# Five padded count matmuls in another bank, and a full-height bias matmul, in a fused attention and mixture-of-experts kernel

## What is computed

```python
x = x + _layernorm(_L0_attn_ref(_layernorm(x), Wq, bq, Wk, bk, Wv, bv, gamma))
x = x + _layernorm(_L0_ffn_ref(_layernorm(x), W1, b1, W2, b2, gate_W, shared_W, shared_b, gamma, beta))
# attention, linear: Q, K normed over the tokens
Q = x @ Wq.T + bq;  K = x @ Wk.T + bk;  V = x @ Wv.T + bv
matrix = einsum('bmn,bcn->bmc', K, V)
matrix_sum = value_sum + einsum('bnm,bmc->bcn', Q, matrix)
# feed-forward: every token goes to its best 2 of 8 experts, and through a shared layer
probs = softmax(flat @ gate_W);  topk_w, topk_idx = top_k(probs, 2)
out = 0.5 * gelu(flat @ shared_W + shared_b)
for e in range(8):
    out = out + combine[:, e:e+1] * (gelu(flat @ W1[e] + b1[e]) @ W2[e] + b2[e])
```

## Time and profile before

| what | value |
|---|---|
| median of the three runs | 714.06 us |
| span of the profiled execution | 750.8 us |
| TensorE busy | 647.7 us (86%) |
| VectorE busy | 458.5 us (61%) |
| ScalarE busy | 460.2 us (61%) |
| GpSimd busy | 299.9 us (40%) |
| mean granted TensorE clock | 0.938 of full |

### The profile page before, as it was taken

One profiled execution on the slowest core, in us unless ns is written; L12 is line 12 of the kernel. 1 busy time (PEld: TensorE's weight loads), 2 busy tenths in 40 slices (PEclk: granted clock), 3 DMA queues, 4 the chain that ended last, 5 costly groups with the idle time before them and its releaser, 6 DMA issues.

```text
span 750.8 us, 17408 instructions
## 1 busy us (share of the span) xinstructions
PE 647.7 (86%) x5255; PEld 547.4 (73%) x5255; DVE 458.5 (61%) x1243; ACT 460.2 (61%) x879; POOL 299.9 (40%) x389
## 2 busy tenths in 40 slices
PE   4779789889887799987988999999999998999930
PEld 3567567667765587866867889998998997887820
DVE  4479878797887563523345544444444445777777
ACT  2657647557555483743555666766675555788975
POOL 4000332432526612464572434544453564534421
PEclk9989999898998899988898999999999999999985
DMA  7563553550155332111112122222111396433567
GB/s 254 170 252 111 172 167 101 182 170 31 61 166 198 85 114 71 44 45 57 37 52 81 59 69 79 84 74 72 58 51 44 78 200 141 78 66 60 115 166 140
DMA packets 46600, 79.88 MB, mean 106 GB/s; under 512 B 17905, under 2 KB 31538, under 8 KB 46130
## 3 DMA queue, kind: packets, MB, share of 16 engines
q1 hardware_dynamic: 33954, 47.17, 19.7%
q0 software_dynamic: 12560, 31.60, 17.9%
HBM read 48.96 MB, written 29.78 MB: 105 GB/s over the span
## 4 chain that ended last, share of the span: by engine, by line
PE 65%; DVE 12%; issue 9%; ACT 8%; DMA 2%; another core or an unknown queue 2%; POOL 1%; ACTq 1%; DVEq 1%; POOLq 0%
PE banks L479 15%; PE banks L480 14%; PE banks L481 14%; PE banks L916 4%; PE banks L850 4%; ACT X L1390 3%; PE banks L869 2%; PE banks L873 2%; DMA X<-y_rows 2%; PE banks L990 2%; PE banks L950 1%; PE banks L899 1%; DVE st L1916 1%; PE banks L934 1%
## 5 line engine op out<-in xcount | busy, mean ns | idle before, releaser
L1390 ACT ACTIVATE X<-banks,b1T,tab 128x256 f32<-128x256 f32 x312 | 157.3, 553 | 144.9 <-PE banks L481 110.2
L1859 DVE SCALAR_TENSOR_TENSOR stage<-X,tab,stage 128x512 f16<-128x512 f32 x156 | 115.7, 751 | 121.0 <-ACT stage L1395 75.9
L479 PE MATMUL banks<-X,W 128*128 128x256 f16 x624 | 172.0, 276 | 10.7 <-DVE X L1866 6.4
L479 PE MATMUL banks<-W,stage 128*128 x624 | 173.0, 277 | 7.2 <-issue 5.7
L753 POOL DMA_INDIRECT y_rows<-X,tb x78 | 87.6, 1123 | 224.0 <-DVE X L1882 209.8
L480 PE MATMUL banks<-W,stage 128*128 x624 | 173.0, 277 | 3.2 <-issue 3.2
L481 PE MATMUL banks<-W,stage 128*128 x624 | 173.1, 277 | 2.8 <-issue 2.7
L480 PE MATMUL banks<-X,W 128*128 128x256 f16 x624 | 171.8, 275 | 0.0
L481 PE MATMUL banks<-X,W 128*128 128x256 f16 x624 | 171.7, 275 | 0.0
L1395 ACT ACTIVATE stage<-X,tab 128x512 f16<-128x512 f32 x156 | 112.6, 722 | 11.3 <-ACT X L1390 7.0
L742 POOL DMA_INDIRECT X<-xf_rows,tb x78 | 89.7, 1149 | 32.4 <-issue 24.8
(11 more groups left out here) (284 smaller groups left out, 1025.3 us busy)
## 6 DMA issues: line engine op xcount, KB each, us to landing
stage<-in_L_ffn_W SPq DMA_DIRECT2D x10, 1024.0 KB
W<-in_L_ffn_W SPq DMA_DIRECT2D x6, 1024.0 KB, 8.9
X<-in_L_attn_x SPq DMA_DIRECT2D x8, 512.0 KB
out<-X SPq DMA_DIRECT2D x8, 512.0 KB
xf_rows<-zone SPq DMA_DIRECT2D x8, 512.0 KB
u_rows<-b2b SPq DMA_DIRECT2D x8, 512.0 KB
X<-y_rows POOLq DMA_DIRECT2D x8, 512.0 KB
away<-W SPq DMA_DIRECT2D x1, 2048.0 KB, 7.5
```

The source lines that it names most:

```text
L479: pe.matmul(o, lh, rh, start=first, stop=False)
L1390: a.activation(h32[:, m % 2, r * BT:(r + 1) * BT], PS[m][:, r * BT:(r + 1) * BT], ACT.Gelu, bias=b1T[:, bass.ds(e * NH + 2 * m + r, 1)], s ...
L1859: v.scalar_tensor_tensor(o[1], src, tab[:, 1, bass.ds(e, 1)], o[0], ALU.mult, ALU.subtract).then_inc(h_low, 1)
```

## The change

The counts are made by five matmuls of 40 columns. The marks now lie in the middle of `both_wide`, four blocks of eight zero columns ahead and one behind. The first matmul puts `upper` against the four tiles and the zero block behind them; each of the next four puts `ones16` against the same 40 columns moved left by one tile more, so that the moved copies add up to the earlier tiles, and for the last eight columns to all four. The counts go to bank 0 (`GRAM_PS`) in place of bank 2. So the waits for the counts' copy leave `key_norms` and `totals`, and one comes to `grams` (and to the second transposes of batch 6), which write bank 0.

The bias is added by one matmul over all 128 partitions: `sides` is 128 x 128 of 2048, and `srow` is zero but for the high half in partition 0 and the low half in partition 32. The bias is loaded twice, to partitions 0 and 32, and ScalarE scales both rows.

```diff
@@ shapes @@
-        sbias = setup_buf([1, D], F32)
+        sbias = setup_buf([LOW_ROW + 1, D], F32)
-        srow = bias_buf([1, 2, DE], F16)
-        row2048 = bias_buf([1, P], F16)
+        srow = bias_buf([P, DE], F16)
+        sides = bias_buf([P, P], F16)
-        both = routing_buf([P, T, E], F16)
+        both_wide = routing_buf([P, 2 * T + 1, E], F16)
+        both = both_wide[:, T:2 * T, :]
         def count_bank(b):
-            return SMALL_PS if b + 2 < B else LATE_PS
+            return GRAM_PS if b + 2 < B else LATE_PS
@@ SyncE, GpSimd: setup @@
-                sp.dma_start(sbias, shared_b.unsqueeze(0)).then_inc(weights_in, 16)
+                for row in (0, LOW_ROW):
+                    sp.dma_start(sbias[row:row + 1, :], shared_b.unsqueeze(0)).then_inc(weights_in, 16)
-            g.memset(row2048, SX).then_inc(units_set, 1)
+            g.memset(sides, SX).then_inc(units_set, 1)
+            g.memset(both_wide, 0.0).then_inc(routing_consts, 1)
@@ TensorE @@
             def grams(b):
                 pe.wait_ge(u_ready, past(T * (b - 2)))
+                pe.wait_ge(counts_ready, past(b - 2))
             def key_norms(b):
                 pe.wait_ge(totals_ready, min(b, E - 1))
-                pe.wait_ge(counts_ready, past(b - 1))
             def shared(b, n):
-                for k in range(2):
-                    mm = pe.matmul(o, row2048, srow[:, k, :], start=False, stop=(k == 1))
-                mm.then_inc(shared_ps, 1)
+                pe.matmul(o, sides, srow, start=False, stop=True).then_inc(shared_ps, 1)
             def totals(i):
-                pe.wait_ge(counts_ready, past(i - 1))
             def count(b):
                 if b + 2 < B:
-                    pe.wait_ge(totals_ready, b + 2)
-                    pe.wait_ge(norms_ready, 2 * (b + 2))
+                    pe.wait_ge(u_ready, T * (b + 1))
-                for t in range(T):
-                    o = small[:, COUNT_AT + t * E:COUNT_AT + (t + 1) * E]
-                    for n in range(t):
-                        pe.matmul(o, ones16[:, :], both[:, n, :], start=(n == 0), stop=False)
-                    pe.matmul(o, upper[:, :], both[:, t, :], start=(t == 0), stop=True)
-                o = small[:, COUNT_AT + T * E:COUNT_AT + (T + 1) * E]
-                for n in range(T):
-                    mm = pe.matmul(o, ones16[:, :], both[:, n, :], start=(n == 0), stop=(n == T - 1))
+                marks = both_wide.rearrange("p t e -> p (t e)")
+                pe.matmul(small[:, 0:(T + 1) * E], upper[:, :], marks[:, T * E:(2 * T + 1) * E], start=True, stop=False)
+                for n in range(1, T + 1):
+                    mm = pe.matmul(small[:, 0:(T + 1) * E], ones16[:, :], marks[:, (T - n) * E:(2 * T + 1 - n) * E], start=False, stop=(n == T))
@@ ScalarE: setup @@
-            a.activation(srow[:, 0, 0:D], sbias, ACT.Copy, scale=scl[0:1, 0:1]).then_inc(shared_high, 1)
+            for row in (0, LOW_ROW):
+                a.activation(srow[row:row + 1, 0:D], sbias[row:row + 1, :], ACT.Copy, scale=scl[row:row + 1, 0:1]).then_inc(shared_high, 1)
```

More of the change, by code:

```diff
@@ L23 @@
 SETUP_V = 14
+LOW_ROW = 32
 EV_BOUNDS, EV = 4, 9
@@ L243, in sandwich @@
         SHARED_PS = [PS[0], PS[1]]
-        NORM_AT, COUNT_AT, EXPERT_AT = 0, 8, 8 + (T + 1) * E
+        NORM_AT, EXPERT_AT = 0, 8
         blocks_ready = sem("blocks_ready")
@@ L928, in turn_xf @@
                     pe.wait_ge(gram_ready, min(b + 3, B))
+                    if b == B - 2:
+                        pe.wait_ge(counts_ready, B - 2)
                 else:
@@ L1047, in _ @@
             pe.matmul(SMALL_PS[:, 0:3], ones32[:, :], ssq[:, 0:3], start=True, stop=True).then_inc(setup_sums, 1)
-            pe.wait_ge(weights_in, 80)
+            pe.wait_ge(weights_in, 96)
             pe.transpose(Z_PS[:, 0, 0:E * NH], b1_n, ident32[0:E * NH, 0:E * NH]).then_inc(b1_turned, 1)
@@ L1055, in _ @@
             pe.wait_ge(units_set, 3)
+            pe.wait_ge(shared_high, 4)
             pe.wait_ge(shared_low, 3)
@@ L1236, in counts_out @@
                 settle(a)
-                a.activation(counts[:, 0:(T + 1) * E], count_bank(b)[:, COUNT_AT:COUNT_AT + (T + 1) * E], ACT.Copy).then_inc(counts_ready, 1)
+                a.activation(counts[:, 0:(T + 1) * E], count_bank(b)[:, 0:(T + 1) * E], ACT.Copy).then_inc(counts_ready, 1)
             def w2_square(i):
@@ L1332, in _ @@
             a.wait_ge(consts_set, 6)
-            a.wait_ge(weights_in, 80)
+            a.wait_ge(weights_in, 96)
             a.activation(dump[:, 0:NF * D], sh_n.rearrange("p j i -> p (j i)"), ACT.Square, accum_out=ssq[:, 0:1]).then_inc(setup_squares, 1)
@@ L1337, in _ @@
             a.wait_ge(setup_squares, 2)
-            a.activation(dump[0:1, 0:D], sbias, ACT.Square, accum_out=ssq[0:1, 2:3]).then_inc(setup_squares, 1)
+            a.activation(dump[0:1, 0:D], sbias[0:1, :], ACT.Square, accum_out=ssq[0:1, 2:3]).then_inc(setup_squares, 1)
             a.wait_ge(setup_steps, 10)
@@ L1604, in pick_experts @@
                 v.wait_ge(u_ready, T * (b + 1))
-                v.wait_ge(routing_consts, 5)
+                v.wait_ge(routing_consts, 6)
                 v.wait_ge(counts_ps, b)
@@ L1833, in _ @@
             v.wait_ge(wv_sums_ps, 1)
-            v.wait_ge(weights_in, 80)
+            v.wait_ge(weights_in, 96)
             v.tensor_scalar(vsum, COS_PS[:, 0:D], gam_b[:, 0:1], None, ALU.mult).then_inc(vsum_ready, 1)
-            v.wait_ge(shared_high, 3)
+            v.wait_ge(shared_high, 4)
             v.scalar_tensor_tensor(sgs[:, :, 1, 0:D], sh_n, scl[:, 0:1], sgs[:, :, 0, 0:D], ALU.mult, ALU.subtract).then_inc(shared_low, 1)
             v.scalar_tensor_tensor(sgs[:, :, 1, D:DE], gate_n, scl[:, 1:2], sgs[:, :, 0, D:DE], ALU.mult, ALU.subtract).then_inc(shared_low, 1)
-            v.scalar_tensor_tensor(srow[:, 1, 0:D], sbias, scl[0:1, 0:1], srow[:, 0, 0:D], ALU.mult, ALU.subtract).then_inc(shared_low, 1)
+            low = slice(LOW_ROW, LOW_ROW + 1)
+            v.scalar_tensor_tensor(srow[low, 0:D], sbias[low, :], scl[low, 0:1], srow[low, 0:D], ALU.mult, ALU.subtract).then_inc(shared_low, 1)
             v.wait_ge(wide_set, 2)
```

## The result

The changed kernel takes **702.05 us** (median of 4 runs, 701.53 to 702.56) against 713.51 us (712.02 to 717.2) for the one before in the same comparison: a ratio of 0.9828, with a 95% interval of 0.9811 to 0.9845. The forecast was 704.0 us in a range of 700 to 712, so both the figure and the direction held. How it came about is another matter: the profile on which the forecast's largest term rested was not like the timed runs, and the closeness of the number is in part luck.

What follows compares the result with a forecast made beforehand. First stage bound by a chain of waits through the counts' copy, second by TensorE; 6.4 + 0.9 + 0.2 + 0.4 + 1.3 + 1.3 - 0.4 = 10.1 us off 714.06 gives 704.0 us, range 700 to 712.

Steps and rivals of the forecast that it cites:

- The wait of `key_norms` goes: First-stage steps: `key_norms` no longer waits for the counts' copy; 6.4 us in steps 3 to 6, 0.9 in step 2.
- the case of a prompt signal: Steps 3 to 6: if the counts' signal comes at once, `norms` waits for TensorE, 1.17 us behind `key_norms`; gain 2.2 us.
- I take 1.6 us for steps 3 to 6, the row as it is: Counts' copy: signal still 1.93 us late, `norms` at 108.43 instead of 110.06; 1.6 us per step, 6.4 us in all.
- rival 2: Late count signal belongs only to the profiled execution; steps 3 to 6 give 1.0 us each, total 706.6 us; chance 0.2.
- The bias in steps 1 to 6: Shared tiles before `attend`: at most 0.2 us per step, taken as 0 because VectorE bounds the next `products`.
- The price of the bias matmul: Shared layer: one full-height matmul costs 0.11 us against the pair's 0.44, weight load hidden; 0.33 us saved per tile.
- Last step and second stage: Last step: 0.2 us from counts, 1.3 from bias; second stage: 0.4 from shorter counts, 1.3 from batch 7's bias tiles.
- The setup: Before step 0: ScalarE scales a second bias row, so everything starts 0.4 us later.
- The floor of a step: First-stage step at full clock: VectorE can give at most 2.80 us of 27.36, so about 24.56 us remain.
- The signs: Expected in the new profile: `key_norms` 0.15 us behind `products`, `norms` 0.1 behind the copy, steps 3 to 6 1.6 shorter.
- Rivals 1 and 4: Late count signal: 1, the count's own work, 700.5 us, chance 0.15; 4, later without TensorE's pause, about 723 us, chance 0.08.
- Rival 3: First stage: half-clock stretches and VectorE eat the gains, leaving 2 to 4 us, about 711 us; chance 0.14.

Runs made afterwards that it cites:

- the second profile: The kernel before, profiled once more with no edit: 715.19 us, with a span of 713.5 us where the first profile had 750.8.

## Why the prediction was right, point by point

- **The wait of `key_norms` goes, and it is the largest part: right.** Moving the bank alone gives 8.8 of the 11.5 us, what the clock gives back included. In the kernel after, `key_norms` starts right behind `products` (101.18 + 0.68 = 101.86; 101.91), and `norms` 1.20 us behind it, against the forecast's 1.17 for the case of a prompt signal.
- **"I take 1.6 us for steps 3 to 6, the row as it is": the mean is right, the reason is wrong.** The 1.6 us stood on the copy that comes late. In the second profile, which has the span of the timed runs, it doesn't: rival 2 had the cause, with its 1.0 us per step, and the counts alone measured 25.83 - 24.75 = 1.1. That steps 3 to 6 still gave 1.6 each on the mean is luck: 1.1 by the wait, 0.2 by the bias and 0.3 by the clock, the last two of which the sum held to be nothing. For want of these two rival 2's 706.6 us was too high as well. The five steps from 2 to 6 gave 7.7 us where the forecast had 7.3: 5.4 by the wait (its own term for rival 2: 4.9), 1.0 by the bias, 1.3 by the clock.
- **The bias in steps 1 to 6: forecast 0 ("at most 0.2 us per step"), measured about 0.2 each**, 0.18 in step 1 already; 25.83 to about 25.6 without the counts' change, 24.75 to 24.55 with it. The forecast held that the next `products` are bound by VectorE anyway. But the chain of waits of the second profile does not go through `products` there. From VectorE's L1597 at 169.57 us it runs through all four tiles of `shared`, `attend`, `turn_x` and `weigh` to ScalarE's copies of `uq`, and so on to the counts. What holds the saving to 0.2 of the four tiles' 1.3 us is what the forecast said: with the bias alone `attend` waits 0.26 us for VectorE's `mixT`, where it had not waited.
- **The price of the bias matmul: right.** 0.11 us, with the weight load hidden. The rule of the Trainium skill (TensorE: Matmul & The Clock Gate, "The mechanism" in Part 3), by which a weight load overlaps with running matmuls only where its row group differs, does not hold for these: L955 starts 0.12 us behind its neighbour and the next 0.11 behind it.
- **Last step and second stage: forecast 1.5 and 1.7 us, together 3.2; measured 1.1 + 2.6 - 0.3 = 3.4.** Their clocks differ too (0.78 to 0.89, 0.93 to 0.96), so this agreement is not a proof of any of the terms. Five matmuls in the place of fourteen gave nothing by themselves (0.9998), with an interval of 2.6 us either way, so of the 0.4 us that they were given nothing is shown.
- **The setup: forecast 0.4 us, measured 0.65** more from the bias to the copy of `b1T` on ScalarE. Whether it reaches the end is open: taking it out of TensorE's way let step 0 start 0.8 us earlier, but step 0 grew by 1.1, at a lower clock. The sign that the forecast named, `weigh` of step 0 later by 0.4 us, can't be read from two profiles: the two of the kernel before differ by 1.1 us themselves (21.48 and 22.57), with 22.54 after.
- **The floor of a step: right.** 27.36 - 2.80 = 24.56 forecast, 24.53 measured, and VectorE there without a wait but one of 0.21 us; 1.3 us more of work on it cost 1.1. The late signal does not spoil this term: in the second profile VectorE waits 0.47 and 0.71 us in step 2, and 25.74 less these is 24.56 again.
- **The signs.** `key_norms` right behind `products` and the bias matmul at 0.11 us came as forecast. Two did not: `norms` stands 0.43 us behind the counts' copy, not 0.1, for it waits for TensorE as in the case of a prompt signal; and at equal clock the steps are 1.3 us shorter, not 1.6 (25.83 to 24.55).
- **Rivals 1 and 4 fell**: the delay is as long behind five matmuls as behind fourteen, and as long when TensorE goes on as when it pauses. **Rival 3 fell too**, the other way round: in the profiles compared the half-clock stretches went with the wait instead of eating the gain.

What stays open: what makes the signals late, and what brings the clock down in those steps. That it goes with the counts' wait is seen in these profiles, one for each kernel, but not isolated.

## What to carry to other kernels

Before a wait is priced from one profile, the profile's span is to be held against the timed runs: where it is 5% longer, as here, profile the kernel once more before an "unknown releaser" is put into a sum. A small result that shares a bank of TensorE's output memory (PSUM) with the next small result is worth a look at what waits for its copy: another bank gave 8.8 us of 714, and the nine matmuls saved gave nothing that could be measured. Where a saving is called hidden, follow the chain of waits of the whole step before taking it as nothing: 0.2 of the 1.3 us of the four tiles came through in each step here. And where one engine bounds a step, look how close the next one is before moving work to it: 0.4 us less on VectorE shortened the step by 0.05.

## What the runs showed of the hardware

- **TensorE's signals came late on one chip of three.** The same kernel took 714 us on two chips and 760 us on another, 6% more. On the latter ScalarE and VectorE stand idle behind an unknown releaser although by the record TensorE has ended: at one of the second stage's copies the transposes end at 501.90 us and VectorE starts at 503.89. By the semaphore times in the traces, 72 to 85 of TensorE's 421 signals are over 0.5 us late in each of the four profiles from this chip, and none in the eight profiles from the other two chips or in that of the kernel after; there they follow the recorded end by 0.01 to 0.02 us (a few signals in each profile have no time that can be matched). The first profile of before, with 56, is like the slow chip's. The views by line of VectorE's copies of the second stage's transposes, the columns being busy, mean ns, and idle before: first the kernel before in its second profile, then the changed kernel with the copy of `b1T` first, on the chip of 760 us.

```profile
L1866 DVE COPY X<-banks 128x1024 f16<-128x1024 f16 x39 | 26.7, 684 | 5.1 <-PE banks L990 5.0
```

```profile
L1867 DVE COPY X<-banks 128x1024 f16<-128x1024 f16 x39 | 26.9, 689 | 71.0 <-remote 65.4 <-PE banks L988 5.5
```

  65.4 us of idleness, ahead of 23 of the 39 copies, 2.8 us each on the mean, that the other two chips do not have; the copies themselves are equally fast. What makes these signals late was not found, nor whether it is the signal or the matmul itself that is late.
- **Forty columns cost no more than eight.** The four matmuls of L976 take 0.25 us and the eight-column ones of L978 0.24; by the starts in the traces both follow one another by 25 ns.
- **Two one-row matmuls among full-height ones cost more than one full-height matmul of the same width**: 0.44 us against 0.11, and the full-height matmul behind the pair takes 0.22 us of the chain where its neighbours take 0.11. In the second profile the weight load of the pair and the one behind it each stand idle for 0.22 us first; those between full-height matmuls do not.
